# A fused two-layer gated cross-attention block: the weighted values moved ahead of the second and third query projection in TensorE's order

## The reference, cut to what matters

```
x = x + tanh(g_xattn[0]) * cross_attention_0(layernorm(x), ctx)     # rotary q, k; mask by length
x = x + tanh(g_ffn[0])   * mixture_of_16_experts(layernorm(x))
x = x + tanh(g_xattn[1]) * cross_attention_1(layernorm(x), ctx)     # rms-normed q, k
x = x + tanh(g_ffn[1])   * lora_of_4_experts(layernorm(x))

# both attentions: 32 query heads in 8 groups of 4, one key and value head per group, head width 128
q = x @ Wq;  k = ctx @ Wk;  v = ctx @ Wv
out = softmax(q k^T / sqrt(128)) v @ Wo        # per sequence of 64 tokens
```

## Time and profile before

| what | value |
|---|---|
| median of 3 runs | 1320.96 us (1320.8 to 1322.37) |
| profiled execution, device time | 1322.38 us |
| its span | 1320.5 us |
| granted PE clock, mean | 0.975 |
| PE busy | 1239.6 us, 94% |
| DVE, POOL, ACT busy | 805.0, 609.8, 493.7 us |
| steps of layer 0's attention | about 210 to 620 us of the span |
| steps of layer 1's attention | about 815 to 1247 us |

### The profile page before, as it was taken

The page is one execution under the profiler, slowest core; times in us unless marked ns, Lnnn a source line. Parts: engine busy times, 40 slices in busy tenths (PEclk is TensorE's granted clock), DMA queues, the critical chain, the costliest instruction groups (busy, mean ns, idle before and its releaser), DMA issues.

```text
span 1320.5 us, 17058 instructions
## 1 busy us (share of the span) xinstructions
PE 1239.6 (94%) x6288; PEld 974.4 (74%) x6288; DVE 805.0 (61%) x1405; ACT 493.7 (37%) x763; POOL 609.8 (46%) x408
## 2 busy tenths in 40 slices
PE   7999998699999999998799999899999999999886
PEld 6877876477777777776587887577777777777665
DVE  4645537987888788888843134645544445544586
ACT  4244132122222212222342124655555565556522
POOL 4421523567867678676242111335354453544400
PEclk9999999899999999999799999899999999999987
DMA  7752746211121111212010003202122112111001
GB/s 255 233 189 96 234 149 239 72 40 72 72 79 72 51 68 64 79 40 96 1 57 32 1 0 125 80 9 104 40 71 71 48 64 79 71 40 41 33 0 64
DMA packets 56098, 106.74 MB, mean 81 GB/s; under 512 B 3377, under 2 KB 36145, under 8 KB 50673
## 3 DMA queue, kind: packets, MB, share of 16 engines
q1 hardware_dynamic: 55520, 105.04, 22.7%
q0 software_dynamic: 384, 1.05, 0.2%
q10 hardware_dynamic: 144, 0.00, 0.0%
HBM read 78.81 MB, written 27.26 MB: 80 GB/s over the span
## 4 chain that ended last, share of the span: by engine, by line
PE 69%; DVE 12%; POOL 8%; issue 6%; ACT 4%; DMA 0%; POOLq 0%; ACTq 0%; DVEq 0%
PE ps_b L213 11%; PE ps_b L215 11%; PE ps_b L214 11%; PE ps_q L213 10%; PE ps_q L215 9%; PE ps_q L214 9%; PE ps_s L816 3%; PE ps_b L835 2%; PE ps_s L802 2%; POOL qT L1010 2%; POOL wo_lo L1005 1%; POOL wq_lo L647 1%; POOL s_sb L679 1%; PE ps_s L255 1%; DVE o_lo L1151 1%
## 5 line engine op out<-in xcount | busy, mean ns | idle before, releaser
L213 PE MATMUL ps_b<-wo_hi,o_hi 128*128 128x512 f32 x512 | 204.5, 399 | 18.9 <-POOL wo_lo L1005 15.7
L213 PE MATMUL ps_q<-hT_hi,wq_hi 128*128 128x512 f32 x512 | 212.4, 415 | 6.5 <-DVE q_t L1085 5.0
L214 PE MATMUL ps_q<-hT_lo,wq_hi 128*128 128x512 f32 x512 | 203.2, 397 | 0.0
L215 PE MATMUL ps_q<-hT_hi,wq_lo 128*128 128x512 f32 x512 | 203.2, 397 | 0.0
L214 PE MATMUL ps_b<-wo_lo,o_hi 128*128 128x512 f32 x512 | 202.3, 395 | 0.0
L215 PE MATMUL ps_b<-wo_hi,o_lo 128*128 128x512 f32 x512 | 202.2, 395 | 0.0
L213 PEld LDWEIGHTS ps_q<-hT_hi,wq_hi 128*128 128x128 f32 x512 | 96.8, 189 | 51.0 <-issue 21.4
L213 PEld LDWEIGHTS ps_b<-wo_hi,o_hi 128*128 128x128 f32 x512 | 97.9, 191 | 42.8 <-issue 18.9
L1160 DVE SCALAR_TENSOR_TENSOR x_sb<-ps_b,gates,x_sb 128x512 f32<-128x512 f32 x128 | 92.4, 727 | 59.0 <-PE ps_b L215 58.4
L1151 DVE TENSOR_TENSOR o_lo<-ps_b,o_hi 128x512 fp32r<-128x512 f32 x128 | 82.2, 684 | 75.5 <-ACT o_hi L942 75.0
L1010 POOL TENSOR_TENSOR qT<-q_t 128x512 f32<-128x512 f32 x64 | 89.8, 1407 | 68.8 <-DVE q_t L1085 68.8
(11 more groups left out here) (240 smaller groups left out, 2471.1 us busy)
## 6 DMA issues: line engine op xcount, KB each, us to landing
wq_raw<-in_wq SPq DMA_DIRECT2D x16, 1024.0 KB, 4.8
wo_raw<-in_wo SPq DMA_DIRECT2D x16, 1024.0 KB, 4.8
v_hi_spill<-vs_hi SPq DMA_DIRECT2D x16, 512.0 KB, 5.9
v_lo_spill<-vs_lo SPq DMA_DIRECT2D x16, 512.0 KB, 6.7
kT_spill<-kT_st SPq DMA_DIRECT2D x4, 2048.0 KB, 7.5
kT<-kT_spill SPq DMA_DIRECT2D x32, 256.0 KB, 3.8
v_hi<-v_hi_spill SPq DMA_DIRECT2D x16, 512.0 KB, 3.7
v_lo<-v_lo_spill SPq DMA_DIRECT2D x16, 512.0 KB, 4.6
```

The costliest lines, as they stand in the source:

```text
L213: nc.tensor.matmul(dst, l_hi, r_hi, start=first, stop=False)
L214: nc.tensor.matmul(dst, l_hi, r_lo, start=False, stop=False)
L215: return nc.tensor.matmul(dst, l_lo, r_hi, start=False, stop=last)
```

## The change

In `step` of `att_pe` the call of `values` moves from behind `project(g, h, 2)` to directly behind `score`. PE's step becomes P0, S, V, P1, P2, P3, O0 to O3 (in layer 1 with SQ in front). Nothing else is changed: no instruction is added or taken away, and the lists of the other engines and their waits are the same.

```diff
--- before.py
+++ after.py
@@ -859,6 +859,8 @@
                     project(g, h, 1)
                 if do_score:
                     score(us, 1 - h, g if h else g - 1)
+                if do_finish:
+                    values(up, h, g - 1)
                 if do_project:
                     if not first_scores(lay, g, h):
                         project(g, h, 1)
@@ -869,8 +871,6 @@
                     if at_first:
                         ln_turn(pe, lns[2], PAIRS + 2)
                         ln_turn(pe, lns[2], PAIRS + 3)
-                if do_finish:
-                    values(up, h, g - 1)
                 if do_project:
                     project(g, h, 3)
                 for t in range(PAIRS):
```

## The result

The kernel with the change takes 1349.78 us in the median (1349.38 to 1350.39, 4 runs), the kernel before 1321.66 (1320.8 to 1322.66, 4 runs): a ratio of 1.0213 [1.0195, 1.0231]. It is slower by 28.1 us; 24.2 were forecast (1345.2 us).

A forecast was written before the change was run, and what follows sets the result against it. PE bounds the kernel, softmax and split chains 0.5 to 1 us behind. 6.1 + 7.0 + 4.4 + 0.75 + 5.9 = 24.2 us on 1322.38 gives 1346.6, as median 1345.2 us; range 1332 to 1354.

The forecast's parts named there:

- surely early: ACT's `o_hi` in layer 0, expected done before P2 ends, with `o_lo` still behind rotate 2; no size given.
- Odd steps of layer 0: O0 waits for `o_lo` behind rotate 2: 0.80 us later plus 0.07, seven steps x 0.87 = 6.1 us.
- Step (1, 0): Layer 0: P1 and P2 no longer fill V's wait for `p_lo`; 2.2 us plus 2.2 for the clock, 4.4 us.
- Its clock term: Step (1, 0), behind PE's 9.7 us standstill: half clock costs 1.7 us plus 0.5 for P1's start, 2.2 more.
- V behind layer 0's last step: V there already waits 1.64 us for `p_lo` and moves with DVE's chain, not PE's 0.87: 0.75 us.
- S to V: The new change of array shape from S to V: taken at 0.2 us, bounds 0 and 0.4.
- Even steps of layer 0: O0 waits 0.79 us more for `wo_lo`, V 0.37 for `p_lo`: six steps x 1.16 = 7.0 us.
- the rival with a chance of 0.08: Granted clock falls in each of six even steps of layer 0, 2.2 us each: 13 us, 1358.4 us; chance 0.08.
- Layer 1: `o_hi` behind head 2's queries delays O0: odd steps 5.5 us, even -0.8, three other steps 1.2; 5.9 us.
- the gain of 0.16 in the even steps: Layer 1's even steps in the loop, where P2 starts late: 5 x (-0.23 + 0.07) = -0.8 us.
- the 0.15 us that the forecast took for a signal: Time from the end of an awaited instruction to PE's start, 0.15 us, read from `wo_lo` and O0.
- The two rules: PSUM bank rotation: O0 starts without a wait, time falls. Tiling-mode drain: one fewer per step is the whole effect.

The follow-up runs named there:

- moved-list kernels: Kernel with the change plus readers' lists reordered, such as ACT's `o_hi` ahead of head 2's queries in layer 1: 1336.44 us.
- the first experiment: Kernel with the change, plus POOL's fourth `wo_lo` ahead of rotation sum 2 in even steps of layer 0: 1337.92 us, 1.0131.
- the readers' lists in layer 0: Kernel with the change, plus POOL's fourth `wo_lo` ahead of rotation sum 2, DVE's `o_lo` 0 and 1 ahead of rotate 2, ACT's `o_hi` sooner: 1337.14 us.

## Why the prediction was right, and where it missed

**The direction and the mechanism** held: O0 is held by what stands behind P2 in the readers' lists. It was shown by moving the lists: POOL's alone (two kernels), ACT's alone in layer 1, DVE's and ACT's together in layer 0. Which of the latter two counts there was not tried apart. One reading of the prediction was wrong here: it had ACT's `o_hi` "surely early" and done before P2 ends. In odd steps of layer 0 they begin at 403.26, behind `wq_hi` 2 and so behind P2. DVE's rotate 2, until 404.88, is later still and sets `o_lo`, which is why the number held; with DVE's list moved alone `o_lo` could have begun some 0.5 us sooner and no more, an estimate from these rows (two of the four `o_hi` are done at 403.26 + 2.04 / 2 = 404.28). The place relative to P2 is what counts (V between P1 and P2).

**Odd steps of layer 0**, forecast at 0.80 + 0.07 = 0.87 each, took 0.89: 13.01 - 12.21 = 0.80 up to O0, and 0.09 behind it. **Step (1, 0)** came to 4.7 for 4.4. Its clock term was right in kind: V to P1 takes 255.98 - 253.12 = 2.86 us instead of 1.62. **V behind layer 0's last step** moved by 0.74 for 0.75. **S to V** was taken at 0.2 us as for the other changes of shape: V begins 1.88 us behind S, just as P1 did, and the saved change is worth 0.2 us in the moved-list kernels.

**Even steps of layer 0: the clock was mis-sized.** The wait for `p_lo` (0.44 for 0.37) and the one for `wo_lo` (2.1 for 2.2) were right, and a step with a full clock lost 1.13 us on average for 1.16. The step that failed is the rival's "Against it: in the stretch with the pause of 3.34 us the granted clock was 1.00". The earlier trace rows end at 255; the window 3 us further on in the same trace of the kernel before reads:

```profile
258.00:261.00 3.00, 3.00 (x9) 2.31 (x8) 2.94 (x5) 0.00 (x0) 2.10 (x2) 0.50 0.00 0
```

There P3 stands behind a second pause, of 2.81 us, and takes 261.75 - 257.32 = 4.43 us instead of 2.9. So that stretch spoke for the rival and not against it. V back in its place in step (1, 0) had a pause of 3.13 us and the low clock at once. In the changed kernel the clock fell in three of six even steps, 1.6 us each, 4.8 in all. That is the rival with a chance of 0.08, at a third of its price of 13 us. The long wait is needed for it: with 0.44 and 1.04 us in a step (the first experiment), or 1.2 in the kernel before, the clock never fell between 300 and 600 us, with 2.1 or 1.9 it did in half of the steps, shortening 1.89 to 0.89 took it away, and taking away the 0.44 ahead of the 2.1 (V between P1 and P2) did not. Why only half of them fall was not found; which half they are changed with nothing but step (1, 0).

**Layer 1** lost 7.2 us for 5.9. The pair of an odd and an even step of the loop went from 28.09 + 28.64 = 56.73 to 29.03 + 28.72 = 57.75, 1.02 more, where 0.92 - 0.16 = 0.76 was forecast; steps (1, 0), (7, 0) and (7, 1) gave 0.35, 0.37 and 0.43 for 0.40. The term at fault is the gain of 0.16 in the even steps; it came out as 0.08 of loss. Nearly all of these 0.24 us lie in the 0.15 us that the forecast took for a signal. O0 begins 0.15 us behind the end of `o_lo` in odd steps, but 0.36 in the even steps of the loop (1002.34 to 1002.70, and in the first experiment 427.83 to 428.19 in layer 0). There PE has two more waits in its list, for `wo_hi` and `wo_lo`, both met long before. In the steps (1, 0) and (7, 0), written out with the same four waits, it is 0.10 (887.11 to 887.21, and 1233.34 to 1233.44), so by these rows the cost goes with those two waits inside the loop; an edit that would show it was not run.

**What came back** was not forecast: 3.0 us between and behind the layers, where no line was changed. The larger part is the clock again. The twelve matmuls of the first group behind layer 0's second set of values begin in the kernel before at 652.15 and in the one after at 676.07, both behind a wait of 0.79. The windows over them, first the kernel before:

```profile
652.00:657.40 5.40, 5.25 (x13) 4.08 (x14) 3.81 (x10) 2.03 (x3) 0.00 (x0) 0.50 0.00 0
```

and after:

```profile
676.00:679.40 3.40, 2.96 (x12) 2.17 (x12) 3.29 (x9) 1.95 (x3) 0.00 (x0) 1.00 0.00 0
```

At 0.50 they need 5.2 us, at 1.00 they and the wait behind them 3.4. That is the 1.8 us between the layers. Of the 1.2 behind layer 1, the like group there gives 0.5 (1279.10 - 1274.26 = 4.84 us before, 1307.84 - 1303.47 = 4.37 after, the granted clock mixed in both); the rest was not traced. Without these 3.0 us the sum would have missed by 7 us instead of 4; that it came so close is in part luck.

**The two rules.** The Trainium skill, "Perfetto Trace Analysis", section Optimizing Tensor Performance, advises to rotate matmul groups through PSUM banks so that evacuation overlaps the next group. In the changed kernel the trace disagrees, since 13.01 - 12.21 = 0.80 us per odd step are lost; it agrees once the readers' lists let it, with O0 at 12.01 and no wait. By the Trainium skill, "TensorEngine Tiling (Array Packing)", section Key Properties, a change of tiling mode drains TensorE. The runs agree that a change costs, 0.2 us for each one saved; that it is a drain no row here shows.

## What to carry to other kernels

Before work is moved within the list of the engine that bounds a kernel, look at who reads it: the readers run their lists in order too, and an early result is read only at its place. Move the reader with it (one line on ACT turned a loss of 7.2 us in layer 1's fourteen steps, 400.40 against 393.24, into a gain of 5.5, 387.73), and first look for readers that are already late, because one such line on POOL was worth 8 us without the change. Put a piece of work earlier only where its own input has a margin: V had that in layer 1, and not for `p_lo` in layer 0's even steps.

## What the runs showed of the hardware

- The granted clock of TensorE fell in three of six even steps behind pauses of 2.1 us at O0 (the kernel after, V between P1 and P2), for 1.6 us of loss each time, and in three of six behind pauses of 1.8 to 1.9 us at V (the readers' lists in layer 0), for 0.9. Behind waits of 0.4 to 1.2 us it never fell there. In step (1, 0) it was 1.00 right behind a pause of 3.34 us and 0.50 behind the next one of 2.81 (the kernel before), and it was 0.50 right behind one of 3.13 (V back in its place).
- Four 32x32 copies between partitions on DVE took 0.73 us alone and 1.75 us beside one 128x512 `TENSOR_TENSOR` on POOL; moving POOL's instruction brought 0.73 back.
- A matmul began 0.15 us behind the end of the DVE instruction that it waited for, or 0.36 us where two more waits, long met, stood behind that one in the loop (0.10 with the same waits written out).
- A stretch with the same code, behind the same wait of 0.79 us, took 1.8 us more in one kernel than in the other, at a granted clock of 0.50 against 1.00.
